# First attention of a four-layer gated model: averages of normalised tokens with folded value and output weights, keys first in each step

## The chip, the cores and the metric

The kernel is one program on one core of a Trainium2 chip. A core has TensorE (matmuls), VectorE, ScalarE and GpSimd (POOL in the profile), and SyncE (SP), which here only issues transfers. Each runs its own instructions in order, and they wait for each other on semaphores. Matmul results go to PSUM, 8 banks of 512 float32 values per partition; everything else stands in SBUF, 128 partitions. The metric is the device time of the whole program in microseconds; lower is better.

## What is computed

`x` is 128 sequences of 64 tokens of width 128, `ctx` has the same shape, all float32. Four layers follow each other, each a gated cross attention and a gated feed-forward:

```python
x = x + tanh(g_xattn[0]) * L0_xattn(ctx, layernorm(x), ...)
x = x + tanh(g_ffn[0])   * L0_ffn(layernorm(x), ...)
...
```

The change touches the first line. Its attention takes, per sequence, queries from 64 latents (the normalised `x`) and keys and values from 128 tokens (64 of `ctx`, 64 latents):

```python
xn = layer_norm(ctx, gamma_x, beta_x)         # context tokens
ln = layer_norm(layernorm(x), gamma_l, beta_l)  # latents
q = ln @ Wq                                   # 8 heads of 64
k = rope(xn @ Wk) for context tokens, ln @ Wk for latents
v = concat(xn, ln) @ Wv
out = softmax(q k^T / 8) v @ Wo               # 512 -> 128
```

Rotation (rope) of a key needs each half of a head's 64 values multiplied by the cosine, and the other half, with a sign, by the sine.

## The kernel before

Tokens are worked in 64 tiles; a tile is two sequences (`PAIR`, index b), 128 tokens on 128 partitions. `flamingo` runs `prepare` (loads and weight preparation) and then eight stages, each a loop over tiles written per engine. The stage of the change is `attention0`. All of `x` stays in SBUF (`k.x`); each stage adds to it in place, and the next stage starts when all tiles of the one before are updated.

Within a stage `steps(engine, T, lead, lag, body)` writes the software pipeline: `body(at)` is called once per step s, and `at(k)` gives the tile s + k (or nothing outside the range). Between a few written-out steps at either end it is a loop of two steps. So the order of the work on each engine is the order of the `if t := at(k)` blocks in its `body`, written out by hand, and a wait such as `pe.wait_ge(*s["krot"](t))` holds everything behind it on that engine. `t.has(2)` and `t.back(2)` name the tile two before, whose buffer or bank is used again.

In a step of `attention0` before:

- SP loads the context tile s+3 (L459), stores the latents' second affine image z1T (L462) and the transposed context (L464) of tile s+1 for a later attention, and swaps partition halves of the keys with two transfers of 64 rows, `kr` from `kc` (L469).
- POOL makes variance plus epsilon and its power -0.5 for tile s+2 (L483, L484, L487).
- TensorE: scores of s (L502), the normalised heads of s-1 turned (L510), keys (L518) and queries (L524) of s+1, three transposes of s+2 (L534 to L536), output product of s-1 (L540), weights of s turned (L550), values of s+1 (L559), weights times values of s (L569). The last has an added column of ones, so that each head's sum of weights comes with it.
- VectorE: statistics of s+2 (L583 to L588), reciprocal and normalising of the heads of s-1 (L592, L594), maximum of the scores and their difference (L602, L604, once per b), xhat (L217, in the helper `tile_xhat`) and zhat (L610) of s+2, keys times cosine (L616), three affines of the turned tokens (L626), the update of x (L630), queries into a block form with zeros `QBD` (L636), keys times sine (L642) and the sum into `KT` (L645).
- ScalarE: exponentials (L656, one per b), copies out of PSUM: `oT` (L661), `kc` (L666), `KT` of the latents (L670), the turned context (L676), the turned weights (L680), the values (L685).

Heads stand in `wq0` and `wk0` with their halves rearranged by VectorE in `prepare`, so that one swap of partition halves serves two heads.

## Time and profile before

| | |
|---|---|
| median of 3 runs | 2354.29 us (2352.95 to 2356.11) |
| the profiled execution, its own time | 2353.34 us |
| its span, first to last instruction | 2351.0 us |
| TensorE busy in the span | 2061.7 us (88%) |
| VectorE | 1836.1 us (78%) |
| ScalarE | 1189.1 us (51%) |
| GpSimd | 263.0 us (11%) |
| mean granted TensorE clock | 0.945 of 2.4 GHz |

The span is the time from the first to the last instruction of one execution on the chip; its own time lies 2.3 us above it. A float32 matmul appears as two records (x16 for 8 matmuls). The recorded busy time of a matmul includes its way through the array, which overlaps the next one; so groups are better read from start to start. `x128` is a count, `<-` in a name reads "from", and at the end of a line stands how long the engine had been idle and what released it.

### The profile page before, as it was taken

What the parts mean: (1) busy time and instruction counts of PE and PEld (TensorE: products, weight loads), DVE (VectorE), ACT (ScalarE), POOL (GpSimd) and SP (SyncE); (2) the same over time, 40 slices, a digit from 0 to 9 for tenths busy, and PEclk for the clock granted to TensorE, in tenths of its full rate; (3) what the DMA queues carried; (4) which work ended last, traced back from release to release, by engine and by line L of the source; (5) the groups of instructions that cost most, each with busy time, mean ns of one, the idle gap of its engine ahead of it and who ended that gap; (6) DMA issues with size and microseconds to landing.
All of it is one profiled execution on the core that took longest, in us unless ns stands there. A gap on an engine that the chain in (4) does not pass through costs nothing. (4 is left out here: it accounts for less than half of the span.)

```text
span 2351.0 us, 51476 instructions
## 1 busy us (share of the span) xinstructions
PE 2061.7 (88%) x17149; PEld 1603.8 (68%) x17149; DVE 1836.1 (78%) x4821; ACT 1189.1 (51%) x2276; POOL 263.0 (11%) x552
## 2 busy tenths in 40 slices
PE   3999999999977999999998978799999985599507
PEld 3888888888867986777775756477777764244207
DVE  3898899889867978888886778567666578787885
ACT  2454555555442217767765645445444445318647
POOL 0111101111101101111101124000000022100000
PEclk8999999999998999999998989799999998799859
DMA  6111111111114541111100011221221110002532
GB/s 181 44 45 47 47 47 47 45 44 44 47 26 186 233 165 26 23 23 25 24 19 1 0 33 42 84 97 72 86 94 72 73 46 28 1 0 107 189 133 71
DMA packets 121398, 153.68 MB, mean 65 GB/s; under 512 B 45513, under 2 KB 102242, under 8 KB 117218
## 3 DMA queue, kind: packets, MB, share of 16 engines
q1 hardware_dynamic: 115320, 149.92, 19.9%
q10 hardware_dynamic: 5994, 2.70, 0.4%
q8 instruction: 45, 0.74, 0.1%
q14 instruction: 39, 0.32, 0.0%
HBM read 110.11 MB, written 25.69 MB: 58 GB/s over the span
## 5 line engine op out<-in xcount | busy, mean ns | idle before, releaser
L1726 DVE TENSOR_TENSOR arena<-arena 128x512 f32<-128x512 f32 (+1 forms) x256 | 171.2, 687 | 64.4 <-ACT arena L1764 61.2
L1764 ACT ACTIVATE arena<-banks,b1c 128x512 f32<-128x512 f32 x192 | 131.7, 687 | 168.3 <-PE banks L1639 168.1
L656 ACT ACTIVATE arena<-arena 128x512 f32<-128x512 f32 x128 | 80.7, 630 | 192.9 <-DVE arena L604 192.9
L1649 PEld LDWEIGHTS banks<-w2a,arena 128*128 128x128 f32 x1024 | 124.1, 192 | 28.7 <-issue 28.7
L909 PE MATMUL banks<-we,arena 128*128 128x128 f32 x1024 | 132.9, 285 | 3.4 <-DVE arena L973 0.5
L502 PE MATMUL banks<-arena 128*128 128x128 f32 x1024 | 131.3, 281 | 0.1
L909 PEld LDWEIGHTS banks<-we,arena 128*128 128x128 f32 x1024 | 123.9, 197 | 10.2 <-DVE arena L973 9.6
L1214 ACT ACTIVATE arena<-arena 128x512 f32<-128x512 f32 x128 | 80.7, 631 | 98.5 <-DVE arena L1166 98.5
L1092 PE MATMUL banks<-arena 128*128 128x512 f32 x256 | 126.0, 615 | 3.9 <-ACT arena L1220 0.3
L1160 DVE TENSOR_REDUCE arena<-banks 128x8 f32<-128x512 f32 x128 | 87.8, 686 | 51.5 <-PE banks L1092 51.4
L518 PE MATMUL banks<-arena,wk 128*128 128x128 f32 x1024 | 126.3, 277 | 1.1 <-DVE arena L626 1.1
L559 PE MATMUL banks<-wv,arena 128*128 128x512 f32 x256 | 123.0, 603 | 2.0 <-ACT arena L676 2.0
L1649 PE MATMUL banks<-w2a,arena 128*128 128x128 f32 x1024 | 124.7, 275 | 0.0
L502 PEld LDWEIGHTS banks<-arena 128*128 128x128 f32 x1024 | 119.1, 191 | 5.3 <-DVE arena L645 0.9
L518 PEld LDWEIGHTS banks<-arena,wk 128*128 128x128 f32 x1024 | 120.8, 194 | 1.5 <-DVE arena L626 1.5
L1639 PE MATMUL banks<-arena,w1s 128*128 128x512 f32 x256 | 121.7, 610 | 0.0
L1854 PE MATMUL banks<-konst,local_max 128*1 128x128 f32 (+1 forms) x4 | 1.4, 346 | 119.6 <-DVE local_max L1838 119.6
L217 DVE TENSOR_SCALAR xhat<-x_tiles,mean_var,rstd 128x128 f32 (+1 forms) x256 | 78.8, 339 | 32.0 <-POOL rstd L762 26.7
L762 POOL TENSOR_TENSOR rstd<-var_eps,konst 128x4 f32<-128x4 f32 x96 | 100.2, 1044 | 15.0 <-POOL var_eps L759 11.6
L759 POOL TENSOR_SCALAR var_eps<-mean_var 128x4 f32<-128x4 f32 x96 | 22.5, 234 | 704.7 <-DVE mean_var L739 702.5
L569 PEld LDWEIGHTS banks<-arena 128*64 128x64 f32 x2048 | 65.0, 137 | 48.8 <-issue 47.8
L626 DVE TENSOR_SCALAR arena<-banks,affine_columns 128x128 f32<-128x128 f32 x192 | 67.0, 404 | 36.5 <-PE banks L536 36.4
(273 smaller groups left out, 5254.1 us busy)
## 6 DMA issues: line engine op xcount, KB each, us to landing
arena<-coef_scratch SPq DMA_DIRECT2D x32, 2048.0 KB, 7.0
arena<-arena SPq DMA_DIRECT2D x128, 128.0 KB, 2.3
gated_scratch<-arena SPq DMA_DIRECT2D x16, 768.0 KB, 3.2
arena<-gated_scratch SPq DMA_DIRECT2D x16, 768.0 KB, 4.3
arena<-z1T_scratch SPq DMA_DIRECT2D x128, 64.0 KB, 2.2
arena<-ctxT_scratch SPq DMA_DIRECT2D x32, 256.0 KB, 2.8
arena<-in_ctx SPq DMA_DIRECT2D x64, 64.0 KB, 1.8
z1T_scratch<-arena SPq DMA_DIRECT2D x64, 64.0 KB, 1.5
```

Source lines behind the costliest of these rows:

```text
L502: mm = pe.matmul(ps[:, 6 + b, c * P:(c + 1) * P], QBD[:, c, b].rearrange("p h i -> p (h i)"), KT[:, c, :, b, :], start=True, stop=True)
L518: mm = pe.matmul(ps[:, n, c * P:(c + 1) * P], k.wk0[:, c * P:(c + 1) * P], Z[t.par][:, :, n], start=True, stop=True)
L559: mm = pe.matmul(ps[:, 4 + b, :], Z[t.par][:, b].rearrange("p s i -> p (s i)"), k.wv0[:, :], start=True, stop=True)
L656: act.activation(prob[:, b], prob[:, b], ACT.Exp, scale=HD0 ** -0.5).then_inc(s["prob"].sem, 1)
L762: pool.tensor_tensor(k.rstd[:, :, 0], k.ve[:, :, 0], k.konst[:, C_MHALF:C_MHALF + GROUP], ALU.pow).then_inc(f["rstd_ready"].sem, GROUP)
L909: mm = pe.matmul(ps[:, OUT + g.par, j * D:(j + 1) * D], xs[g.par][:, n, j * P:(j + 1) * P], k.we0[:, n, :], start=n == 0, stop=n == EXPERT ...
L1092: pe.matmul(ps[:, 3 + n, :], QB[t.par][:, n].rearrange("p b i -> p (b i)"), KM[t.par][:, n].rearrange("p h i -> p (h i)"), start=True, sto ...
L1160: dve.tensor_reduce(mx[:, n], ps[:, 3 + n, :].rearrange("p (h i) -> p h i", i=SEQ), AX.X, ALU.max)\
L1639: pe.matmul(ps[:, HID + c % NHID, :], w, xTg[g.par], start=True, stop=True).then_inc(s["h_psum"].sem, 1)
L1649: mm = pe.matmul(ps[:, OUT + g.par, j * D:(j + 1) * D], hT[g.par][:, c, j * P:(j + 1) * P], w, start=c == 0, stop=c == CHUNKS2 - 1)
L1726: dve.tensor_tensor(hT[g.par][rows, c, :], hT[g.par][rows, c, :], wide_coef[g.par][rows, e, :], ALU.mult).then_inc(s["scaled"].sem, 1)
L1764: act.activation(hT[g.par][:, c, :], ps[:, HID + c % NHID, :], ACT.Gelu, bias=k.b1c[:, c:c + 1])\
```

## The change

`attention0` is rewritten, with what it needs in `prepare`:

- Values are no longer computed per tile. Per head, Wv Wo is folded once at the start (`wvo0`, 8 products of 128 by 128). Per tile the normalised tokens (both kinds, `Z`) are turned back into rows (`zn`), the softmax weights average them (two products of 512 columns, result `Y`), and eight accumulating products with `wvo0` give the output.
- The weights are normalised before they are turned: a sum, a reciprocal and a multiplication on VectorE. The exponentials read the scores in PSUM with minus the maximum as the bias operand, one instruction per head pair.
- Keys come first in TensorE's step. `KT` has a second buffer. The output product of s-1 goes to bank 0 (`KC`), where the next step's first key product goes too; VectorE updates x with it as the first thing of the next step (`steps(dve, T, 2, 2, body)`).
- The z1T affine is made on ScalarE. `QBD` is cleared once by POOL and filled by two ScalarE copies.
- The keys' halves are no longer rearranged in the weights; the swap is of neighbouring blocks of 32 rows, four transfers.
- The transposed context is an input made on the host (`ctxT`), and so is the transposed Wv (`wvT`); the stage no longer turns or stores the context.

The diff, cut to its core (removed lines of the bodies are in the listing above):

```diff
+    gates_raw = raw(8)
+    k.wq0, k.wk0 = (sb(n, [P, INNER]) for n in ("wq0", "wk0"))
...
+        (k.wq0[:, :], a["L0_xattn_Wq"]), (k.wk0[:, :], wkv[:, 0:INNER]), (wvT, a["wvT"]),
+        (wo_raw, a["L0_xattn_Wo"].rearrange("(c p) d -> p c d", p=P)),
         (k.we0[:, :, :], a["L0_ffn_We"].rearrange("e d m -> d e m")),
...
         act.activation(k.bout[:, :], ps[:, 7, D:2 * D], ACT.Copy, scale=k.gates[:, 2:3]).then_inc(folded_sb, 1)
+        act.wait_ge(folded, 3)
+        for n in range(2):
+            act.activation(k.wvo0[:, n::2, :], ps[:, n, :].rearrange("p (h d) -> p h d", d=D), ACT.Copy)\
...
         pe.matmul(ps[:, 7, D:2 * D], k.konst[0:1, C_ONES:C_ONES + P], bo_row[0:1, :], start=False, stop=True)\
             .then_inc(folded, 1)
+        for h in range(H0):
+            rows = slice(h % 2 * HD0, h % 2 * HD0 + HD0)
+            mm = pe.matmul(ps[:, h % 2, h // 2 * D:(h // 2 + 1) * D], wvT[rows, h // 2, :], wo_raw[rows, h // 2, :],
+                           start=True, stop=True)
...
+    mx, nb, ssum, rec = (k.take(PAIR * HPAIRS).rearrange("p (b c) -> p b c", b=PAIR) for _ in range(4))
+    prob = k.take(PAIR * 512).rearrange("p (b c n) -> p b c n", b=PAIR, c=HPAIRS)
+    probT = k.take(PAIR * 512).rearrange("p (b n) -> p b n", b=PAIR)
...
         def body(at):
             if t := at(3):
                 if t.has(2):
+                    sp.wait_ge(*s["zhat"](t.back(2)))
+                    k.hold(sp)
                 sp.dma_start(cin[t.par], ctx_dram[t.idx]).then_inc(ctx_loaded.at(t), 16)
             if t := at(1):
                 sp.wait_ge(*s["kc"](t))
+                k.hold(sp)
                 if t.has(1):
                     sp.wait_ge(*s["ksin"](t.back(1)))
+                    k.hold(sp)
+                for n in range(4):
+                    to, of = n * 32, (n ^ 1) * 32
+                    sp.dma_start(kr[to:to + 32, :], kc[of:of + 32, :]).then_inc(swapped.at(t), 16)
+                sp.wait_ge(*s["z1"](t))
+                k.hold(sp)
+                sp.dma_start(k.z1T_dram[t.idx], z1o[t.par]).then_inc(k.z1T_stored.at(t), 16)
...
+        pool.memset(QBD, 0.0).then_inc(preset, 1)
...
+        def body(at):
+            if t := at(1):
+                if t.has(3):
+                    pe.wait_ge(*f["x_updated"](t.back(3)))
+                if t.has(1):
+                    pe.wait_ge(*s["klat"](t.back(1)))
+                for n in range(2):
+                    pe.wait_ge(*s["z_ready"](t, n + 1))
+                    for c in range(HPAIRS):
+                        mm = pe.matmul(ps[:, KC + n, c * P:(c + 1) * P], k.wk0[:, c * P:(c + 1) * P], Z[t.par][:, :, n],
+                                       start=True, stop=True)
+                    mm.then_inc(s["k_psum"].sem, 1)
+            if t := at(-1):
+                for b in range(PAIR):
+                    pe.wait_ge(*s["normed"](t, b + 1))
+                    if t.has(1):
+                        pe.wait_ge(*s["y_sb"](t.back(1), b + 1))
+                    for c in range(HPAIRS):
+                        mm = pe.transpose(ps[:, PT + b, c * P:(c + 1) * P], prob[:, b, c], k.ident)
+                    mm.then_inc(s["pt_psum"].sem, 1)
             if t := at(0):
                 pe.wait_ge(*s["krot"](t))
                 pe.wait_ge(*s["klat"](t))
                 pe.wait_ge(*s["qbd"](t))
+                if t.has(1):
+                    pe.wait_ge(*s["prob"](t.back(1)))
                 for b in range(PAIR):
                     for c in range(HPAIRS):
+                        mm = pe.matmul(ps[:, S + b, c * P:(c + 1) * P], QBD[:, c, b].rearrange("p h i -> p (h i)"),
+                                       KT[t.par][:, c, :, b, :], start=True, stop=True)
                     mm.then_inc(s["s_psum"].sem, 1)
+                if at(1):
+                    pe.wait_ge(*s["z1"](at(1)))
+                for b in range(PAIR):
+                    mm = pe.transpose(ps[:, TURN, (2 + b) * P:(3 + b) * P], Z[t.par][:, b].rearrange("p s i -> p (s i)"),
+                                      k.ident)
+                mm.then_inc(s["zn_psum"].sem, 1)
             if t := at(-1):
+                pe.wait_ge(*s["zn_sb"](t))
+                for b in range(PAIR):
+                    pe.wait_ge(*s["pt_sb"](t, b + 1))
+                    pe.matmul(ps[:, PT + b, :], zn[t.par][:, b], probT[:, b], start=True, stop=True)\
+                        .then_inc(s["y_psum"].sem, 1)
+            if t := at(1):
+                if t.has(1):
+                    pe.wait_ge(*s["qbd"](t.back(1)))
                 for c in range(HPAIRS):
+                    mm = pe.matmul(ps[:, Q, c * P:(c + 1) * P], k.wq0[:, c * P:(c + 1) * P], Z[t.par][:, :, 1],
                                    start=True, stop=True)
                 mm.then_inc(s["q_psum"].sem, 1)
             if t := at(2):
                 pe.wait_ge(*f["xhat_ready"](t))
                 pe.wait_ge(*s["zhat"](t))
+                if at(0):
+                    pe.wait_ge(*s["zn_sb"](at(0)))
+                if at(1):
+                    pe.wait_ge(*s["z1"](at(1)))
+                pe.transpose(ps[:, TURN, 0:P], k.xh[:, t.par, :], k.ident)
+                pe.transpose(ps[:, TURN, P:2 * P], zh[t.par], k.ident).then_inc(f["xT_psum"].sem, 1)
             if t := at(-1):
+                pe.wait_ge(*s["y_sb"](t))
                 if at(1):
                     pe.wait_ge(*s["kc"](at(1)))
+                elif t.has(1):
+                    pe.wait_ge(*f["x_updated"](t.back(1)))
                 for h in range(H0):
+                    mm = pe.matmul(ps[:, KC, 0:D], Y[:, h].rearrange("p b i -> p (b i)"), k.wvo0[:, h, :],
+                                   start=h == 0, stop=h == H0 - 1)
...
+        def normalise(t, b):
+            dve.wait_ge(*s["prob"](t, (b + 1) * HPAIRS))
+            dve.tensor_reduce(ssum[:, b], prob[:, b], AX.X, ALU.add).then_inc(s["ssum"].sem, 1)
+            dve.wait_ge(*s["ssum"](t, b + 1))
+            dve.reciprocal(rec[:, b], ssum[:, b]).then_inc(s["srec"].sem, 1)
+            dve.wait_ge(*s["srec"](t, b + 1))
+            dve.tensor_tensor(prob[:, b], prob[:, b], rec[:, b].unsqueeze(2).broadcast_to([P, HPAIRS, P]), ALU.mult)\
+                .then_inc(s["normed"].sem, 1)
+        def body(at):
+            if t := at(-2):
+                dve.wait_ge(*s["out_psum"](t))
+                dve.scalar_tensor_tensor(out=k.x[:, t.idx, :], in0=ps[:, KC, 0:D], scalar=k.gates[:, 0:1],
+                                         in1=k.x[:, t.idx, :], op0=ALU.mult, op1=ALU.add)\
+                    .then_inc(f["x_updated"].sem, 1)
+            if t := at(-1):
+                normalise(t, 1)
...
             if t := at(1):
                 if t.has(1):
                     dve.wait_ge(*s["krot"](t.back(1)))
                 dve.wait_ge(*s["kc"](t))
                 dve.tensor_tensor(rotA.rearrange("p (c i) -> p c i", i=SEQ), kc.rearrange("p (c i) -> p c i", i=SEQ),
...
+            if t := at(0):
+                for b in range(PAIR):
+                    dve.wait_ge(*s["s_psum"](t, b + 1))
+                    dve.tensor_reduce(mx[:, b], ps[:, S + b, :].rearrange("p (c n) -> p c n", c=HPAIRS), AX.X, ALU.max)\
+                        .then_inc(s["smax"].sem, 1)
+                    dve.wait_ge(*s["smax"](t, b + 1))
+                    if t.has(1):
+                        dve.wait_ge(*s["prob"](t.back(1)))
+                    dve.tensor_scalar(nb[:, b], mx[:, b], -HD0 ** -0.5, None, ALU.mult).then_inc(s["nb"].sem, 1)
             if t := at(1):
                 dve.wait_ge(*swapped(t))
                 dve.tensor_tensor(rotB.rearrange("p (c i) -> p c i", i=SEQ), kr.rearrange("p (c i) -> p c i", i=SEQ),
                                   sinT, ALU.mult).then_inc(s["ksin"].sem, 1)
                 dve.wait_ge(*s["ksin"](t))
+                dve.wait_ge(*s["kcos"](t))
+                if t.has(2):
+                    dve.wait_ge(*s["s_psum"](t.back(2)))
+                dve.tensor_tensor(KT[t.par][:, :, 0], rotA.rearrange("p (c b i) -> p c b i", c=HPAIRS, b=PAIR),
                                   rotB.rearrange("p (c b i) -> p c b i", c=HPAIRS, b=PAIR), ALU.add)\
                     .then_inc(s["krot"].sem, 1)
+            if t := at(2):
+                sl = t.par
+                if t.has(2):
+                    dve.wait_ge(*f["xT_psum"](t.back(2)))
+                tile_xhat(k, f, dve, t, sl)
+                dve.tensor_scalar(zh[sl], cin[sl], k.mv[:, sl, 1, 0:1], k.rstd[:, sl, 1:2],
+                                  ALU.subtract, ALU.mult).then_inc(s["zhat"].sem, 1)
+            if t := at(0):
+                normalise(t, 0)
+            if t := at(2):
+                sl = t.par
+                if t.has(2):
+                    dve.wait_ge(*s["zn_psum"](t.back(2)))
+                    dve.wait_ge(*s["q_psum"](t.back(2)))
+                dve.wait_ge(*f["xT_psum"](t))
+                for dst, n, g in ((Z[sl][:, :, 0], 1, 0), (Z[sl][:, :, 1], 0, 2)):
+                    dve.tensor_scalar(dst, ps[:, TURN, n * P:(n + 1) * P].rearrange("p (b i) -> p b i", b=PAIR),
+                                      k.aff[:, g:g + 1], k.aff[:, g + 1:g + 2],
+                                      ALU.mult, ALU.add).then_inc(s["z_ready"].sem, 1)
+        steps(dve, T, 2, 2, body)
...
         def body(at):
             def weights(b):
                 if t := at(0):
+                    act.wait_ge(*s["nb"](t, b + 1))
+                    if t.has(1):
+                        act.wait_ge(*s["pt_psum"](t.back(1), b + 1))
+                    for c in range(HPAIRS):
+                        act.activation(prob[:, b, c], ps[:, S + b, c * P:(c + 1) * P], ACT.Exp, scale=HD0 ** -0.5,
+                                       bias=nb[:, b, c:c + 1]).then_inc(s["prob"].sem, 1)
+            def average(b):
+                if t := at(-1):
+                    if t.has(1) and b == 0:
+                        act.wait_ge(*s["out_psum"](t.back(1)))
+                    act.wait_ge(*s["y_psum"](t, b + 1))
+                    act.activation(Y[:, :, b, :], ps[:, PT + b, :].rearrange("p (h i) -> p h i", i=SEQ), ACT.Copy)\
+                        .then_inc(s["y_sb"].sem, 1)
             if t := at(1):
+                act.wait_ge(*s["z_ready"](t))
+                if t.has(2):
+                    act.wait_ge(*k.z1T_stored(t.back(2)))
+                act.activation(z1o[t.par], ps[:, TURN, P:2 * P], ACT.Identity, scale=k.aff[:, 4:5],
+                               bias=k.aff[:, 5:6]).then_inc(s["z1"].sem, 1)
                 act.wait_ge(*s["k_psum"](t, 1))
                 if t.has(1):
+                    act.wait_ge(*s["kcos"](t.back(1)))
+                    act.wait_ge(*swapped(t.back(1)))
+                act.activation(kc, ps[:, KC, :], ACT.Copy).then_inc(s["kc"].sem, 1)
+                act.wait_ge(*s["k_psum"](t))
+                if t.has(2):
+                    act.wait_ge(*s["s_psum"](t.back(2)))
+                act.activation(KT[t.par][:, :, 1], ps[:, KL, :].rearrange("p (c b i) -> p c b i", c=HPAIRS, b=PAIR),
+                               ACT.Copy).then_inc(s["klat"].sem, 1)
+            if t := at(-1):
+                for b in range(PAIR):
+                    act.wait_ge(*s["pt_psum"](t, b + 1))
+                    act.activation(probT[:, b], ps[:, PT + b, :], ACT.Copy).then_inc(s["pt_sb"].sem, 1)
+            weights(0)
+            average(0)
+            if t := at(0):
+                act.wait_ge(*s["zn_psum"](t))
+                if t.has(2):
+                    act.wait_ge(*s["y_psum"](t.back(2)))
+                act.activation(zn[t.par].rearrange("p b d -> p (b d)"), ps[:, TURN, 2 * P:4 * P], ACT.Copy)\
+                    .then_inc(s["zn_sb"].sem, 1)
+            average(1)
             weights(1)
             if t := at(1):
+                act.wait_ge(*s["q_psum"](t))
+                if t.has(1):
+                    act.wait_ge(*s["s_psum"](t.back(1)))
+                for h in range(2):
+                    rows = slice(64 * h, 64 * h + 64)
+                    act.activation(QBD[rows, :, :, h, :].rearrange("p c b i -> p (c b) i"),
+                                   ps[rows, Q, :].rearrange("p (n i) -> p n i", i=SEQ), ACT.Copy)\
...
+    c[:, C_SIN:C_SIN + SEQ] *= np.where(np.arange(P) // (HD0 // 2) % 2 == 0, -1, 1)[:, None]
     c[:, C_IOTA:C_IOTA + EXPERTS] = np.arange(EXPERTS)
...
-    for name, a in list(inputs.items()) + [("shape_constants", shape_constants())]:
+    tiles = np.asarray(inputs["ctx_1024"]).reshape(-1, P, D)
+    wv = np.asarray(inputs["L0_xattn_Wkv"])[:, INNER:].reshape(D, HPAIRS, P)
+    laid_out = [("shape_constants", shape_constants()), ("ctxT", tiles.transpose(0, 2, 1)),
+                ("wvT", wv.transpose(2, 1, 0))]
+    for name, a in list(inputs.items()) + laid_out:
```

## Rows read from the trace of the kernel before

**Rows 1.** Busy time, engine by engine, with granted clock, DMA share and GB/s.

```profile
60.00:680.00 620.00, 620.00 (x6131) 539.44 (x6131) 556.57 (x1230) 312.49 (x617) 65.91 (x183) 1.00 0.19 46
```

**Rows 2.** TensorE in order of time, one step: start, duration, line, operation.

```profile
409.54 1.92 PE L559 MATMUL banks<-wv,arena 128*128 128x512 f32 x4
411.39 1.15 PE L569 MATMUL banks<-arena 128*64 128x65 f32 x32
412.48 2.05 PE L502 MATMUL banks<-arena 128*128 128x128 f32 x16
414.37 0.60 PE L510 MATMUL banks<-konst,arena 128*128 128x128 f32 x4
414.80 1.95 PE L518 MATMUL banks<-arena,wk 128*128 128x128 f32 x16
416.59 1.06 PE L524 MATMUL banks<-arena,wq 128*128 128x128 f32 x8
...
417.81 1.06 PE L540 MATMUL banks<-wo,arena 128*128 128x128 f32 x8
418.70 1.04 PE L550 MATMUL banks<-konst,arena 128*128 128x128 f32 x8
419.58 1.92 PE L559 MATMUL banks<-wv,arena 128*128 128x512 f32 x4
```

**Rows 3.** VectorE in order of time, from a step of the same stage.

```profile
408.05 1.05 DVE L626 TENSOR_SCALAR arena<-banks,affine_columns 128x128 f32<-128x128 f32 x3 [0.56 <-PE banks L536]
409.01 0.34 DVE L630 SCALAR_TENSOR_TENSOR x_tiles<-banks,gates,x_tiles 128x128 f32 x1
409.27 1.21 DVE L636 TENSOR_TENSOR arena<-banks,konst 128x1024 f32<-128x1024 f32 x1
410.40 0.68 DVE L642 TENSOR_TENSOR arena<-arena,konst 128x512 f32<-128x512 f32 x1
411.12 0.69 DVE L645 TENSOR_TENSOR arena<-arena 128x512 f32<-128x512 f32 x1
411.75 0.29 DVE L583 BATCH_NORM_STATS2 bn_parts<-arena 128x6 f32<-128x128 f32 x1
...
412.59 0.21 DVE L592 RECIPROCAL arena<-banks 128x8 f32<-128x8 f32 x1
```

**Rows 4.** Groups by line and shape, whole span: busy, mean ns, then idle before.

```profile
L602 DVE TENSOR_REDUCE arena<-banks 128x4 f32<-128x512 f32 x128 | 87.7, 685 | 9.5 <-PE banks L502 0.5
L666 ACT ACTIVATE arena<-banks 128x512 f32<-128x512 f32 x64 | 37.7, 589 | 1.8 <-PE banks L518 1.8
L1237 ACT ACTIVATE arena<-banks,affine_columns 128x128 f32<-128x128 f32 x64 | 30.2, 472 | 25.3 <-PE banks L1153 25.3
L350 ACT ACTIVATE bout<-banks,gates 128x128 f32<-128x128 f32 x1 | 0.4, 361 | 0.0
```

**Rows 5.** Transfers: SP's queue in one step, and the page's list (KB, us to landing).

```profile
406.72 1.11 SPq L469 DMA_DIRECT2D arena<-arena  x2
...
arena<-arena SPq DMA_DIRECT2D x128, 128.0 KB, 2.3
```

**Rows 6.** The start of the stage in order of time, TensorE and VectorE.

```profile
43.09 3.49 PE L518 MATMUL banks<-arena,wk 128*128 128x128 f32 x16 [1.14 <-DVE arena L626]
...
50.65 0.69 DVE L645 TENSOR_TENSOR arena<-arena 128x512 f32<-128x512 f32 x1
...
51.40 2.05 PE L502 MATMUL banks<-arena 128*128 128x128 f32 x16
```

**Rows 7.** The end of the stage in order of time, TensorE and VectorE.

```profile
683.01 2.05 PE L502 MATMUL banks<-arena 128*128 128x128 f32 x16
...
693.13 1.16 PE L540 MATMUL banks<-wo,arena 128*128 128x128 f32 x8 [0.69 <-ACT arena L661]
...
694.33 0.35 DVE L630 SCALAR_TENSOR_TENSOR x_tiles<-banks,gates,x_tiles 128x128 f32<-128x128 f32 x1 [2.60 <-PE banks L540]
```

**Rows 8.** A stretch of a later stage, busy times and clock as in the first group.

```profile
1400.00:1420.00 20.00, 17.76 (x163) 14.21 (x162) 19.01 (x83) 12.04 (x23) 9.83 (x12) 1.00 0.19 55
```

More of the change, by code:

```diff
@@ L411, in ready @@
         eng.wait_ge(gates_ready, 2)
[L412 to L413 removed]
+        eng.wait_ge(built, 1)
+        eng.wait_ge(turned_sb, 11)
         eng.wait_ge(folded_sb, 5)
@@ L421, in attention0 @@
 def attention0(k, no):
-    nc, ps, T = k.nc, k.psum, k.T
+    ps, T = k.psum, k.T
     f = k.front(no)
@@ L429, in attention0 @@
     Z = [z.rearrange("p (b s i) -> p b s i", b=PAIR, s=2) for z in two(2 * P)]
-    z1o, cto = two(P), two(P)
-    KT = k.take(HPAIRS * 4 * SEQ).rearrange("p (c s b i) -> p c s b i", c=HPAIRS, s=2, b=PAIR)
+    zn = [z.rearrange("p (b d) -> p b d", b=PAIR) for z in two(PAIR * D)]
+    z1o = two(P)
+    KT = [v.rearrange("p (c s b i) -> p c s b i", c=HPAIRS, s=2, b=PAIR) for v in two(HPAIRS * 4 * SEQ)]
     kc, kr = k.take(512), k.take(512)
@@ L529, in body @@
                 pe.wait_ge(*s["zhat"](t))
-                if t.has(1):
-                    pe.wait_ge(*s["ctxT_sb"](t.back(1)))
-                if t.has(2):
-                    pe.wait_ge(*s["v_sb"](t.back(2)))
-                pe.transpose(ps[:, 4, 0:P], k.xh[:, t.par, :], k.ident)
-                pe.transpose(ps[:, 4, P:2 * P], zh[t.par], k.ident)
-                pe.transpose(ps[:, 4, 2 * P:3 * P], cin[t.par], k.ident).then_inc(f["xT_psum"].sem, 1)
-            if t := at(-1):
-                pe.wait_ge(*s["ot_sb"](t))
-                for c in range(HPAIRS):
-                    mm = pe.matmul(ps[:, 5, 0:D], oT[:, c * P:(c + 1) * P], k.wo0[:, c, :],
-                                   start=c == 0, stop=c == HPAIRS - 1)
-                mm.then_inc(s["out_psum"].sem, 1)
@@ L552, in body @@
-            if t := at(1):
-                if at(2):
-                    pe.wait_ge(*s["z_ready"](at(2)))
-                    pe.wait_ge(*s["ctxT_sb"](at(2)))
-                if at(-1):
-                    pe.wait_ge(*f["x_updated"](at(-1)))
-                for b in range(PAIR):
-                    mm = pe.matmul(ps[:, 4 + b, :], Z[t.par][:, b].rearrange("p s i -> p (s i)"), k.wv0[:, :],
-                                   start=True, stop=True)
-                    mm.then_inc(s["v_psum"].sem, 1)
```

165 lines of the change are left out of this document (16 added, 149 removed).

## The prediction

> **What bounds the kernel now.** I first asked for the busy time of each engine over the stage of the first attention, which is the only stage that the change rewrites. In 620 us of it TensorE is busy 620.00 us, VectorE 556.57, ScalarE 312.49, GpSimd 65.91, at a granted clock of 1.00 (2.4 GHz) [rows 1]. So a step is as long as TensorE's work in it. Next, TensorE in order of time through one step [rows 2]: from one V product (L559) to the next it is 10.04 us, and each group starts when the one before has been issued. VectorE in the same step [rows 3] works about 9 us and waits once, 0.56 us, for the turned tiles (L626). From the first scores (51.40) to the last (683.01) there are 63 steps in 631.61 us [rows 6, 7]: 10.03 us each.
>
> I use start-to-start distances, not busy times: 8 matmuls of 128 columns take 1.79 us (L518), 4 take 0.89, a transpose 0.11 (8 in 0.88, L550), a 512-column matmul 0.925 (L559, 1.85 for two). The tail of a group is recorded 0.17 us past the last distance (1.06 busy against 0.89).
>
> **TensorE's work.** Removed per step: V (1.85), weights times V (L569, 1.09), turning the normalised heads (L510, 0.43), the old output product (0.89), one of the three transposes of tokens (0.11). Added: two transposes of the normalised tokens (0.22), two 512-column products of tokens and weights (1.85), an output product of 8 matmuls instead of 4 (1.78). The scores lose 0.10: L502 takes 1.89 where L518 takes 1.79 for the same shape, and its first matmul comes right after the 64-row products that go. Sum: keys 1.79, weights turned 0.88, scores 1.79, tokens turned 0.22, averages 1.85, queries 0.89, tokens of step+2 turned 0.22, output 1.78: **9.42 us**, 0.61 less than now. Alone that would be 63 x 0.61 = 38 us.
>
> **The wait that takes its place.** The new key product writes bank 0, which also holds the output product of the tile before last. So the first instruction of TensorE's step waits for `x_updated`, VectorE's first instruction of the same step, and that waits for the output product, the last of TensorE's step before. Nothing is between them in TensorE's queue. The price is in the last tile of the stage and the first one: the output product's end at 694.29, the update from 694.33 (0.04 later) for 0.35 [rows 7]; the rotated keys' end at 51.34 and TensorE's next start at 51.40, 0.06 later [rows 6]; and a group after a wait is 0.10 longer (1.16 for 8 records against 1.06) [rows 2, 7]. Tail 0.17 + 0.04 + 0.35 + 0.06 + 0.10 = 0.72 us. TensorE's step is then 9.42 + 0.72 = 10.14, already longer than 10.03. Behind the waiting key product on TensorE's queue stands everything.
>
> **Walking one new step.** Zero is the first key matmul; a handoff is taken as 0.05. First keys done 1.16, ScalarE copies them out (0.59, L666) until 1.80 [rows 4]. TensorE: keys to 1.89, weights turned to 2.77, scores of b=0 to 3.66 (recorded 3.83), b=1 to 4.56 (4.73), tokens turned 4.78, averages 6.63, queries 7.52. It now needs xhat and zhat of tile step+2.
>
> VectorE: the update from -0.41, then the normalising of b=1 (a sum like L602's 0.69 [rows 4], a reciprocal like L592's 0.21, a multiplication like L645's distance 0.63, with 0.04 before each dependent one, as between L642 and L645 [rows 3]), 1.6 us, in time for the transposes of b=1 at 2.33; statistics 0.84; keys times cosine. All done near 3.0; it waits for scores. Maximum of b=0 at 3.88, its negative 0.73 later (4.61, 0.18 like L592's small tile), maximum of b=1 at 4.79, negative at 5.52, free at 5.70. Then keys times sine, which needs the swapped keys; the sum 0.72 later; xhat 0.63 later; zhat 0.26 later for 0.34 [rows 3]. Starting at 5.70, zhat is ready at 7.65 and TensorE, due at 7.52, waits 0.18.
>
> The **swap** is now four DMAs of 32 rows instead of two of 64. SP issues the present two in 1.11 us, and one lands 2.3 us after issue [rows 5]; now they are far from any reader's wait. There is no row for a 32-row one. Lower bound: proportional to rows, 0.28 each, the last landing at 5.0. Upper: 0.56 each, so the last is issued at 1.85 + 1.67 = 3.52 and lands at 5.82, sine at 5.87. I take the upper one, the row's own price per instruction. Then the sum is at 6.59, xhat 7.22, zhat 7.48 to 7.82, TensorE turns them from 7.87 (0.35 idle) to 8.15 (0.06 for starting afresh), output to 9.93 (recorded 10.10), update 10.15 to 10.50, next keys at 10.55. VectorE has normalised b=0 by 9.35 and written Z by 9.99, just before the update. **Step 10.55**; with the swap in time, 10.38.
>
> On this the Trainium skill (DMA: Bandwidth & Descriptors, Rules for kernel authors) speaks against the split: transfers to disjoint partition halves use the same engines, so splitting wins nothing. The rows here show one size only and cannot say it; by that rule the four take at least what the two took, which leaves the step between 10.38 and 10.55.
>
> ScalarE: the exponentials of one b are now 4 instructions instead of one, 0.36 each with a per-partition operand (L350) [rows 4], 1.44; from 4.84 they end 6.3, the copy of averages 0 by 6.9, tokens 7.3, averages 1 at 7.9, before the output product at 8.15. The z1 affine, moved here from VectorE, runs before the keys are done. Queries' copies end near 10.5, wanted by the scores at 13.3. Hidden, with 0.2 us of margin. Lost margin would lengthen the step one for one.
>
> SP: the context load now waits for zhat and still has a step; the z1T store stands behind the four swaps, and its reader is the next attention. The ctxT store (64 KB a tile) is gone, nobody waited for it. POOL's three instructions per tile are unmoved; its one clearing of QBD lies beside the first context load. The four weight copies at the start go (-0.8), but eight folding products (0.43 each at the low clock, as the first key products: 8 in 3.49 [rows 6], 3.4) and two copies (1.1) come at the end of the preparation, of which about 2.5 us is left after the overlap: bounds 1.5 and 3.7.
>
> **Ends of the stage.** Keys of tile 0 start at 43.09, scores at 51.40 [rows 6], 8.3 later. In the new order the first keys are copied out 2.7 after their start (half of 3.49, 0.2, handoff, 0.6), swapped (1.7 and 2.3: 6.8), rotated (8.1), the next tile is normalised and turned (9.1), its affines made and keys computed (11.7): +3.4, less 0.3 for the third affine. The first interval lacks averages and output (-0.3), the last lacks keys (-0.7). Drain: from the last scores 11.7 us now (683.01 to 694.68) [rows 7]; new: scores and averages of the tile before 4, exponentials 1.8, normalising 1.7, transposes and copy 1.2, averages 1.0, copy 0.65, output 1.95, update 0.4, 12.8: +1.1. Sum with the preparation: 2.5 + 3.1 - 1.0 + 1.1 = **5.7 us**.
>
> **The sum.** 63 x (10.55 - 10.03) = 32.8, plus 5.7: +38.5 us on the profiled execution's own 2353.3, **2391.8 us**. The median of the runs shown is 1 us higher. Other stages read the same bytes and stay. A measurement of this kernel can tell 0.2%, 4.7 us, from no change.
>
> **Rivals.**
> Swap in time (the split costs nothing): step 10.38, 2353.3 + 22.1 + 5.7 = **2381**. For it: the low bound of the issue. Chance 0.25.
> Only the handoff at the step's boundary: xhat is never late, 10.14, **2366**. Against it: VectorE's chain behind the scores is 3.8 us of measured durations. 0.10.
> **Faster.** The update is hidden and TensorE's work alone decides: 9.42, 2353 - 38.4 + 5.7 = **2320**. It needs the 0.72 to vanish and xhat early; it decides from a step under 9.86 (10.4 us less over 63 steps, of which the ends take 5.7 and 4.7 are left). Against it: both waits are in the program's order, and VectorE's own distances, read off the walk, already add to 9.3. 0.10. Between that and the handoff case, unchanged within 0.2%: 0.06.
> Heavier: exponentials and averages late on ScalarE (at 0.47 each, L1237's price with two operands [rows 4], the last copy would miss 8.15 by 0.2 us), or register waits between VectorE's many small instructions (0.05 on six of them, 0.3): 10.7 to 10.9, **2400 to 2414 us**, 0.09.
> The clock drops: TensorE now pauses twice a step. The rows are against it: at 17.76 us busy in 20 it stayed 1.00 [rows 8]. Were one step in twenty at the lower level, 1.2 GHz, its 9.4 us of work would double: +30 us on the forecast, **2422**, 0.02. The Trainium skill (TensorE: Matmul & The Clock Gate, A second HAM failure mode: psum-queue depth-cycling) reports a clock that swings with frequent short pauses between groups of matmuls; rows 8 do not show that.
> My forecast: 0.38.
>
> Slower by over 0.2%: 0.38 + 0.25 + 0.10 + 0.09 + 0.02 = 0.84; same 0.06; faster 0.10. The range leaves out the faster case and part of the heavier one, and takes in the bounds of the swap and of the preparation: 2363 to 2406.
>
> **What would show it.** In the new profile: TensorE idle about 0.5 us before the keys, released by the update; idle 0.2 to 0.4 before the transposes of xhat; VectorE idle near 0.9 before the first maximum; sine idle on a DMA (forecast) or never (first rival); ScalarE 7 to 8 us busy per step. If TensorE stays 100% busy, I am wrong on the side of the faster case.

## The result and the profile after

The changed kernel takes 2412.7 us (median of 4 runs, 2409.62 to 2414.02) against 2355.2 us (4 runs): ratio 1.0241, 95% interval 1.0223 to 1.0258. It is slower, as forecast, but by 57.5 us instead of 38.5, and 7 us above the upper end of the range (2406). The profiled execution took 2409.62 us with a span of 2407.8, 56.8 more than before.

First, one step of the changed kernel in order of time. TensorE (start, duration, line, operation, idle before and its releaser):

```profile
402.57 2.05 PE L509 MATMUL banks<-arena,wk 128*128 128x128 f32 x16 [0.75 <-DVE x_tiles L586]
404.45 1.04 PE L518 MATMUL banks<-konst,arena 128*128 128x128 f32 x8
405.32 1.95 PE L528 MATMUL banks<-arena 128*128 128x128 f32 x16
407.11 0.38 PE L534 MATMUL banks<-konst,arena 128*128 128x128 f32 x2
407.33 1.88 PE L541 MATMUL banks<-arena 128*128 128x512 f32 x4
409.05 1.05 PE L547 MATMUL banks<-arena,wq 128*128 128x128 f32 x8
410.56 0.30 PE L557 MATMUL banks<-konst,xhat 128*128 128x128 f32 x1 [0.45 <-DVE xhat L216]
...
410.80 1.95 PE L566 MATMUL banks<-wvo,arena 128*128 128x128 f32 x16
413.39 2.05 PE L509 MATMUL banks<-arena,wk 128*128 128x128 f32 x16 [0.64 <-DVE x_tiles L586]
```

VectorE in the same step:

```profile
401.99 0.35 DVE L586 SCALAR_TENSOR_TENSOR x_tiles<-banks,gates,x_tiles 128x128 f32 x1 [0.29 <-PE banks L566]
...
406.42 0.69 DVE L610 TENSOR_REDUCE arena<-banks 128x4 f32<-128x512 f32 x1 [1.10 <-PE banks L528]
...
408.52 0.69 DVE L618 TENSOR_TENSOR arena<-arena,konst 128x512 f32<-128x512 f32 x1 [0.31 <-DMA arena<-arena]
409.25 0.69 DVE L624 TENSOR_TENSOR arena<-arena 128x512 f32<-128x512 f32 x1
...
410.11 0.34 DVE L632 TENSOR_SCALAR arena<-arena,mean_var,rstd 128x128 f32<-128x128 f32 x1
...
412.90 0.35 DVE L586 SCALAR_TENSOR_TENSOR x_tiles<-banks,gates,x_tiles 128x128 f32 x1 [0.28 <-PE banks L566]
```

TensorE, never idle before [rows 1], pauses twice: 0.45 us before xhat (L557; 0.36 in the next step) and 0.64 or 0.75 us, in turn, before the keys (L509), each time for VectorE. Its groups have the lengths that were added up: from L509 to L518 1.88 with the late first matmul, then 0.87, 1.79, 0.22, 1.72 (forecast 1.85); the issue of the output product (L566) shows only where nothing is waited for behind it, in e1 and e3 below: 1.79 and 1.80. VectorE pauses too, 1.10 us for the scores, 0.31 for the swapped keys (L618), 0.28 or 0.29 for the output product. No engine is full: each waits for the other in turn, which is what a closed chain of waits (one that leads back to its own start, one step later) would look like. Whether it is one, the experiments test.

The busy times of a stretch of the stage (columns as in [rows 1]) and SP's four swap transfers, with their way to landing from the view of that line:

```profile
400.00:500.00 100.00, 89.40 (x665) 77.48 (x663) 81.30 (x205) 66.39 (x166) 12.23 (x27) 1.00 0.15 36
```

```profile
404.66 2.42 SPq L474 DMA_DIRECT2D arena<-arena  x4
```

```profile
L474 SPq DMA_DIRECT2D arena<-arena x256: 507/584/1439, 46.3 to 731.0; - x128
...
DMA to landing us min/median/max: 1.9/2.0/2.9
```

TensorE is down from 100% to 89%, ScalarE up from 50% to 66%, the granted clock stays at 1.00 although TensorE pauses twice a step. Issuing a 32-row transfer costs SP 0.58 us (median 584 ns), as a 64-row one did (two in 1.11 us [rows 5]).

**Where the 56.8 us are.** Scores of tile 0 start at 57.14 us (51.40 before), those of tile 63 at 739.07 (683.01), and x of the last tile is updated at 753.27 (694.68). So 5.7 us come before the first scores, 50.3 over the 63 steps (681.93 against 631.61), 2.5 in the drain; the other stages, whose code is the same, are 1.8 us shorter. From the eighth key product to the 62nd of 64, keys follow keys after 10.81 to 10.90 us; before them, single steps take up to 11.8.

### The profile page after: what moved, and what is told of

Its sections match the earlier page's. It is cut to its first block and busy times, and to the rows that moved or that the text cites. A ratio compares the mean times of both kernels' runs of the same rounds, so it can differ in the third digit from the quotient of the medians.

```text
span 2407.8 us, 49851 instructions
## 1 busy us (share of the span) xinstructions
PE 2048.0 (85%) x15437; PEld 1589.4 (66%) x15437; DVE 1820.7 (76%) x4945; ACT 1327.0 (55%) x2790; POOL 280.0 (12%) x551
## 5 line engine op out<-in xcount | busy, mean ns | idle before, releaser
L659 ACT ACTIVATE arena<-banks,arena 128x128 f32<-128x128 f32 x512 | 146.1, 372 | 70.0 <-DVE arena L615 70.0
L509 PE MATMUL banks<-arena,wk 128*128 128x128 f32 x1024 | 135.5, 287 | 44.2 <-DVE x_tiles L586 41.6
L509 PEld LDWEIGHTS banks<-arena,wk 128*128 128x128 f32 x1024 | 123.3, 197 | 56.5 <-DVE arena L643 52.0
L610 DVE TENSOR_REDUCE arena<-banks 128x4 f32<-128x512 f32 x128 | 88.6, 692 | 72.3 <-PE banks L528 72.3
L1236 ACT ACTIVATE arena<-arena 128x512 f32<-128x512 f32 x128 | 80.7, 631 | 95.2 <-DVE arena L1188 95.2
L1114 PE MATMUL banks<-arena 128*128 128x512 f32 x256 | 125.1, 611 | 1.5 <-ACT arena L1242 0.3
L566 PE MATMUL banks<-wvo,arena 128*128 128x128 f32 x1024 | 125.1, 275 | 1.4 <-ACT arena L667 1.4
L528 PE MATMUL banks<-arena 128*128 128x128 f32 x1024 | 125.4, 276 | 0.0
L566 PEld LDWEIGHTS banks<-wvo,arena 128*128 128x128 f32 x1024 | 119.4, 192 | 3.0 <-ACT arena L667 3.0
L541 PE MATMUL banks<-arena 128*128 128x512 f32 x256 | 120.5, 593 | 0.0
```

Source lines behind the costliest of these rows:

```text
L509: mm = pe.matmul(ps[:, KC + n, c * P:(c + 1) * P], k.wk0[:, c * P:(c + 1) * P], Z[t.par][:, :, n], start=True, stop=True)
L528: mm = pe.matmul(ps[:, S + b, c * P:(c + 1) * P], QBD[:, c, b].rearrange("p h i -> p (h i)"), KT[t.par][:, c, :, b, :], start=True, stop=True)
L541: pe.matmul(ps[:, PT + b, :], zn[t.par][:, b], probT[:, b], start=True, stop=True)\
L566: mm = pe.matmul(ps[:, KC, 0:D], Y[:, h].rearrange("p b i -> p (b i)"), k.wvo0[:, h, :], start=h == 0, stop=h == H0 - 1)
L659: act.activation(prob[:, b, c], ps[:, S + b, c * P:(c + 1) * P], ACT.Exp, scale=HD0 ** -0.5, bias=nb[:, b, c:c + 1]).then_inc(s["prob"].se ...
L1114: pe.matmul(ps[:, 3 + n, :], QB[t.par][:, n].rearrange("p b i -> p (b i)"), KM[t.par][:, n].rearrange("p h i -> p (h i)"), start=True, sto ...
```

## The experiments

All start from the changed kernel except the one that says otherwise. The question was what a step of 10.83 us consists of, since the forecast had 10.55, and whether its two pauses are one chain or two independent losses.

**e1_output_bank: the boundary wait alone.**

```diff
@@ tensor, keys of s+1
-                if t.has(3):
-                    pe.wait_ge(*f["x_updated"](t.back(3)))
@@ tensor, weights of s-1 turned
+                if t.has(1):
+                    pe.wait_ge(*f["x_updated"](t.back(1)))
@@ tensor, output product of s-1
-                if at(1):
-                    pe.wait_ge(*s["kc"](at(1)))
-                elif t.has(1):
-                    pe.wait_ge(*f["x_updated"](t.back(1)))
...
-                    mm = pe.matmul(ps[:, KC, 0:D], Y[:, h].rearrange("p b i -> p (b i)"), k.wvo0[:, h, :],
+                    mm = pe.matmul(ps[:, PT, 0:D], Y[:, h].rearrange("p b i -> p (b i)"), k.wvo0[:, h, :],
```

(The update of x reads `ps[:, PT, 0:D]` too.)

> The changed kernel with one part moved: the output product of a tile goes to the bank of the turned weights (PT, free once the averages of b=0 are copied) instead of the keys' bank, so the key product no longer waits for the update of x; the next turning of the weights does. My theory: a step of the changed kernel (10.83 us) is one closed chain, keys, swap, sine, sum, xhat, zhat, turned tokens, output product, update, keys; its piece from the output product's issue to the next key product (tail 0.17, handoff 0.15, update 0.35, handoff 0.14) goes, the wait for xhat stays. Step 10.0 us, 61 steps save 0.8 each: about 2364 us. Rival (the wait at the boundary only takes the place of a wait for xhat that would come anyway): the pause of TensorE before xhat's transposes grows by what is saved and the step stays over 10.5: 2395 or more.

Measured: 2354.01 us (10 runs, 2348.85 to 2358.16), ratio to the kernel before 0.9994 (0.9983 to 1.0004): 58.7 us below the changed kernel, all that it had lost, and 10 us less than expected. TensorE around the boundary:

```profile
410.92 0.30 PE L557 MATMUL banks<-konst,xhat 128*128 128x128 f32 x1 [0.29 <-DVE xhat L216]
...
411.17 1.95 PE L562 MATMUL banks<-wvo,arena 128*128 128x128 f32 x16
412.96 1.95 PE L507 MATMUL banks<-arena,wk 128*128 128x128 f32 x16
```

The keys now follow the output product after 1.79 us, its issue alone, and the pause before xhat did not grow; it shrank, to 0.29. The step is 9.83 and 9.93 us in turn. The rival falls. The step went below the expected 10.0 because that pause shrank too. The keys, no longer behind a wait, are on their way sooner: SP starts the swap 1.86 us after the first key matmul (404.97 after 403.11) instead of 2.09. The sine then starts 0.32 us after the last minus-maximum instruction, against 0.48 in the changed kernel; without any wait it is 0.12 (e4 below), so the swap is still a little late. A step of 9.88 is already shorter than the 10.03 of the kernel before; the total is the same because the stage's start and end are longer (5.6 us more before the first scores and 2.5 more behind the last, as in the changed kernel).

**e2_xhat_early: the late xhat alone.**

```diff
@@ vector, after nb
+            if t := at(2):
+                sl = t.par
+                if t.has(2):
+                    dve.wait_ge(*f["xT_psum"](t.back(2)))
+                tile_xhat(k, f, dve, t, sl)
+                dve.tensor_scalar(zh[sl], cin[sl], k.mv[:, sl, 1, 0:1], k.rstd[:, sl, 1:2],
+                                  ALU.subtract, ALU.mult).then_inc(s["zhat"].sem, 1)
             if t := at(1):
                 dve.wait_ge(*swapped(t))
...
-            if t := at(2):
-                sl = t.par
-                if t.has(2):
-                    dve.wait_ge(*f["xT_psum"](t.back(2)))
-                tile_xhat(k, f, dve, t, sl)
-                dve.tensor_scalar(zh[sl], cin[sl], k.mv[:, sl, 1, 0:1], k.rstd[:, sl, 1:2],
-                                  ALU.subtract, ALU.mult).then_inc(s["zhat"].sem, 1)
```

> The changed kernel with VectorE's xhat and zhat of tile s+2 placed before the keys times sine, so behind neither the swap nor the rotation. My theory: TensorE no longer waits before the transposes of xhat (0.45 us), the boundary wait stays: step 10.2 us, about 2374 us; the sine no longer waits for the swap. Rival (only the boundary counts): step unchanged, 2412 us. Rival (VectorE is the bound, its order does not matter): unchanged too, with VectorE at no idle.

Measured: 2372.22 us (4 runs, 2370.27 to 2375.74), ratio to the kernel before 1.0077 (1.006 to 1.0094), 40.5 below the changed kernel. TensorE:

```profile
410.14 0.27 PE L557 MATMUL banks<-konst,xhat 128*128 128x128 f32 x1
...
410.36 1.95 PE L566 MATMUL banks<-wvo,arena 128*128 128x128 f32 x16
412.94 2.05 PE L509 MATMUL banks<-arena,wk 128*128 128x128 f32 x16 [0.63 <-DVE x_tiles L586]
```

The pause before xhat is gone, the one before the keys (0.63 and 0.75 in turn) is all that is left, step 10.17 and 10.29. The order on VectorE does matter, against both rivals.

**e4_two_swaps: the price of the split.** Rows 64 to 127 are not swapped.

```diff
-                for n in range(4):
+                for n in range(2):
```

(`keys_swapped` counts two, and POOL clears `kr` once.)

> The changed kernel with two of the four swap transfers left out (rows 64 to 127 of the swapped keys stay zero, so rotated keys of those rows are not those of the reference). My theory: the swap's issue on SP, 0.6 us each, ends later than VectorE is free, and the sine's wait of 0.31 and 0.22 us on alternate steps is on the closed chain: step 0.27 us shorter, about 2396 us. Rival (a swap in time, the wait is absorbed elsewhere): 2412 us.

Measured: 2386.81 us (4 runs, 2382.04 to 2390.93), 25.9 below the changed kernel and 9 below what was expected. The steady steps take 10.45 and 10.56 us, 0.33 less than 10.83; over 61 steps that is 20 us. In the two profiles all 63 steps together are 21.8 us shorter, among them a first one of the changed kernel that takes 11.60 us from sine to sine with a wait of 1.10 for the swap, and the first scores start 1.9 us sooner. Another 3.8 us of the spans' difference lie behind the last scores, where the edit changed nothing. VectorE in this kernel, minus the maximum and then the sine:

```profile
404.51 0.17 DVE L616 TENSOR_SCALAR arena<-arena 128x4 f32<-128x4 f32 x1
404.63 0.69 DVE L619 TENSOR_TENSOR arena<-arena,konst 128x512 f32<-128x512 f32 x1
```

0.12 us apart, no wait. So the last two transfers were on the chain, and the rival of a swap in time falls. This run stands in for a swap by two transfers of 64 rows: two issues of 32 rows take SP 1.15 us, the old pair took 1.11, but the old pair moved twice the bytes and landed 2.3 us after issue instead of 2.0.

**e5_written_out: why the handoffs were longer than forecast.** `steps` writes all 67 steps of the stage out; every wait is then on a constant and there is no loop.

```diff
-    if end - first < 4:
+    if flat or end - first < 4:
@@ attention0, all five engines
-        steps(pe, T, 2, 1, body)
+        steps(pe, T, 2, 1, body, flat=True)
```

> The changed kernel with all steps of the first attention written out instead of a loop of two steps, so that every wait is on a constant. The prediction took 0.05 us for a handoff between engines, from rows outside the loop; inside it the profile of the changed kernel shows 0.11 to 0.15 where an engine stands waiting. Theory A (waits on register values cost it): the handoffs fall back to 0.05, the step from 10.83 to about 10.55, 2395 us. Theory B (handoffs under load are longer whatever the wait): unchanged, 2412 us, and a longer time if fetching more instructions costs.

Measured: 2403.28 us (4 runs, 2400.76 to 2407.98), 9.4 below the changed kernel, less than theory A's 17. One of its steps, TensorE and VectorE, and SP's queue in that step and in the one before:

```profile
410.79 1.95 PE L566 MATMUL banks<-wvo,arena 128*128 128x128 f32 x16
412.78 0.35 DVE L586 SCALAR_TENSOR_TENSOR x_tiles<-banks,gates,x_tiles 128x128 f32<-128x128 f32 x1 [0.16 <-PE banks L566]
413.19 2.05 PE L509 MATMUL banks<-arena,wk 128*128 128x128 f32 x16 [0.44 <-DVE x_tiles L586]
...
419.04 0.69 DVE L618 TENSOR_TENSOR arena<-arena,konst 128x512 f32<-128x512 f32 x1 [0.21 <-DMA arena<-arena]
...
421.32 1.95 PE L566 MATMUL banks<-wvo,arena 128*128 128x128 f32 x16
423.31 0.35 DVE L586 SCALAR_TENSOR_TENSOR x_tiles<-banks,gates,x_tiles 128x128 f32<-128x128 f32 x1 [0.16 <-PE banks L566]
423.72 0.49 PE L509 MATMUL banks<-arena,wk 128*128 128x128 f32 x2 [0.45 <-DVE x_tiles L586]
```

```profile
403.94 3.14 SPq L474 DMA_DIRECT2D arena<-arena  x4
...
415.15 2.41 SPq L474 DMA_DIRECT2D arena<-arena  x4
```

Both theories hold a part. A handoff is the time from the end of one engine's instruction to the start of another's that waits for it. The output product ends at 412.74 and the update starts at 412.78; the update ends at 413.13 and the keys start at 413.19: 0.04 and 0.06 us, the two numbers that the prediction had read outside the loop [rows 6, 7]. In the loop they are 0.15 (412.75 to 412.90) and 0.14 (413.25 to 413.39) in one step and 0.17 (401.82 to 401.99) and 0.23 (402.34 to 402.57) in the other. This step is 10.53 us long. But 19 of 58 steps (the first three and the last two left aside) take 10.8 to 12.0, 15 us more together than at 10.5: in the step from 401.98 to 413.19 the swap took SP 3.14 us, and the sine waited 0.89. Written out, one issue took up to 1.68 us. The transfers that fetch instructions, between 100 and 600 us, first of the changed kernel (queue, packets, MB, share), then written out:

```profile
q14 instruction: 2, 0.02, 0.0%
q8 instruction: 1, 0.02, 0.0%
```

```profile
q8 instruction: 27, 0.44, 0.4%
q14 instruction: 26, 0.21, 0.1%
```

The trace ties the long issues to these fetches. Between 50 and 740 us, 15 of the 376 issues on SP took over 0.8 us, and each of the 15 began within 0.5 us of the start of a 16 KB transfer on q8; of the other 361, none took more than 0.60 us. The changed kernel has two such issues in its first steps, both beside such a transfer; the longer of the two (1.44 us) is behind the wait of 1.10 above. That the fetch makes the issue long is what fits; no run took the fetches away.

Where the longer handoff comes from, the trace shows in part. Two groups of the changed kernel, which this kernel's trace does not have (PEldq is the queue of weight loads, DVEq that of VectorE; durations in ns):

```profile
L507 PEldq FUSED_REGOPS  x58: 37/37/42, 98.1 to 716.6; - x58
L586 DVEq FUSED_REGOPS  x58: 64/70/89, 97.5 to 716.1; - x58
```

There are 58 of each, one for each of the loop's 58 steps. In the loop a register instruction takes the wait (TensorE's at 413.29, 0.04 us after the update's end), and the first weights load behind it, at 413.38; written out, that load itself takes the wait, at 413.19. In every second step, the one that begins the loop's body, TensorE has two register instructions there (402.38 and 402.48, the load at 402.56), and the handoff is 0.23 instead of 0.14. So theory A is right about the size: steps with the swap in time fall from 10.83 to 10.51 us. Late transfers take most of it back.

**e7_before_written_out: the same on the kernel before.** The edit of e5 on the kernel before.

> The kernel before with all steps of its first attention written out. TensorE was never idle there, so register waits cost it nothing: 2354 us, unchanged within 0.2 per cent. If writing out itself costs (fetch of instructions), it shows here as 2360 us or more.

Measured: 2357.68 us (10 runs, 2353.52 to 2360.36), ratio 1.0009 (1.0000 to 1.0019): unchanged within 0.2%. A handoff's wait costs nothing where TensorE is never idle. Writing out is still not quite free: from the first scores to the last the profile shows 635.22 us against 631.61, because each step takes TensorE 10.09 us instead of 10.03, the difference standing around its V product (from L550 to L569 2.79 against 2.72). The kernel before has the same 10.10 in the few steps that it writes out itself.

**e3_bank_and_xhat: both moves.** The diffs of e1 and e2 together.

> The changed kernel with both moves: output product in the bank of the turned weights, xhat and zhat before the sine. Each alone took the step from 10.83 to 9.88 and to 10.17 us. My theory: both pieces of the chain are gone, TensorE's own 9.42 us and a wait of 0.1 to 0.2 for the normalised weights of b=1 are left: step 9.55, about 2335 us, and less than the kernel before. Rival (VectorE, whose distances add to 9.1 and which still hands over four times a step, decides): step 9.7 to 9.9, 2343 to 2355 us, TensorE idle more than 0.3 us a step.

Measured: 2324.16 us (5 runs, 2320.85 to 2330.46), ratio to the kernel before **0.9869** (0.9851 to 0.9887). It beats both. Busy times, then the scores of two neighbouring steps on TensorE:

```profile
100.00:600.00 500.00, 499.36 (x3816) 444.35 (x3815) 461.15 (x1166) 381.79 (x954) 71.49 (x160) 1.00 0.17 42
```

```profile
400.59 1.95 PE L528 MATMUL banks<-arena 128*128 128x128 f32 x16
...
409.99 1.95 PE L528 MATMUL banks<-arena 128*128 128x128 f32 x16
```

TensorE is busy again without a gap (499.36 of 500 us), and from scores to scores it is 9.40 and 9.45 us in turn. The rival in which VectorE decides falls. The two moves alone took 0.95 and 0.60 us off the step, both together 1.41. So the two pauses were pieces of one chain, and what is taken out of it adds up until TensorE's own work decides.

**e6_both_written_out.** e3 and e5 together.

> The kernel with both moves and all steps of the stage written out. Written out, the changed kernel had steps of 10.51 us (the prediction's 10.55) wherever the swap was in time, and steps of 11 to 12 where one issue of the swap on SP took over 1 us. With xhat before the sine the swap is behind more work. My theory: the long issues are mostly covered, the shorter handoffs gain at most 0.05 a step, 2332 to 2340 us. Rival (fetching written-out code costs on every engine): 2345 us or more.

Measured: 2341.05 us (4 runs, 2339.23 to 2341.84), ratio 0.9937 (0.9922 to 0.9953), 17 us above e3 and just above the 2340 that I had allowed. Most steps are 9.46 us, where the loop of e3 has 9.40 and 9.45, and 20 of 63 are 9.85 to 10.6, 14 us more together. All 18 issues on SP over 0.8 us again begin within 0.5 us of a 16 KB instruction transfer, and VectorE then waits for the swap (17 times between 100 and 600 us, 10.2 us in all). Short handoffs gain nothing here. For this kernel the loop is the better form.

**e8_both_two_swaps.** e3 with the edit of e4.

> The kernel with both moves and two of the four swap transfers left out (rows 64 to 127 of the swapped keys stay zero). My theory: the swap is off the chain once xhat does not stand behind it, so the two transfers are worth nothing now: the same time as with both moves alone, within 3 us. Rival (the transfers cost by themselves, by SP's queue or by traffic, wherever the sine stands): 10 to 20 us less.

Measured: 2318.75 us (4 runs, 2316.89 to 2324.61), 5.4 below e3, whose runs overlap it. The steady steps are the same, 9.40 and 9.45. In the two profiles (spans 2322.7 and 2327.1) 4.2 us of the difference lie in the first seven steps, 66.4 against 70.6 us from keys to keys, where the sine still waits with four transfers (0.74 and 0.70 us, and 2.87 against 1.57 for the first tile). So the two transfers cost nothing in the steady state once xhat does not stand behind them, and some 4 us at the start, a little more than I had expected.

## Why the prediction was right in kind and short in size

The walked step, from the key product on, against two neighbouring steps of the changed kernel (keys at 402.57 and at 413.39) and the undisturbed step of e5 (413.19):

| | forecast | changed kernel | its next step | written out |
|---|---|---|---|---|
| SP issues the first swap | 1.85 | 2.09 | 1.96 | 1.96 |
| sine starts | 5.87 | 5.95 | 5.86 | 5.85 |
| zhat done | 7.82 | 7.88 | 7.79 | 7.78 |
| output product starts | 8.15 | 8.23 | 8.14 | 8.13 |
| update of x starts | 10.15 | 10.33 | 10.26 | 10.12 |
| next keys | 10.55 | 10.82 | 10.84 | 10.53 |

**The wait that takes its place** was right: e1 removes it alone and gets all the loss back. Its price was too low, and that is the step of the prediction that failed: the two handoffs at the boundary, taken as 0.04 and 0.06 from the first and last tiles of the stage, which are written out, where the loop has 0.15 and 0.14 in one step and 0.17 and 0.23 in the next. By the table, from the output product to the next keys was forecast as 2.40; it is 2.59 and 2.70 in the loop and 2.40 written out. Up to the output product the walk is 0.08 short in one step and exact in the other. Together the step is 0.27 to 0.29 longer; over 61 steps that is 17 us of the 18 by which the total was too small. A row of the loop was there to read: VectorE's affines [rows 3] began at 408.05, 0.11 after the last transpose before them had ended:

```profile
407.67 0.27 PE L536 MATMUL banks<-konst,arena 128*128 128x128 f32 x1
```

**The swap** came out right at the end that was taken, the sine at 5.95 and 5.86 instead of 5.87, but by two errors that offset each other: SP began it 0.11 to 0.24 later and needed 0.605 us instead of 0.56 for each of the four, and they landed after 2.0 us instead of 2.3. e4 puts the price of two transfers more at 0.33 us a step, where the forecast had 0.17 for the split: the sine moves up by the whole wait. The Trainium skill (DMA: Bandwidth & Descriptors, Rules for kernel authors), cited there, says that splitting over partition halves wins nothing. This case agrees: four issues take SP 2.42 us, two took 1.11.

**TensorE's work**, 9.42 us as a sum of start-to-start distances, is what e3 runs at (9.40). The gain of 0.6 us a step was real all the time. That the sum is so close is partly luck: in e3 the averages take 1.72 instead of 1.85 and the keys 1.89 instead of 1.79. The 0.10 that L502 takes longer than L518 [rows 2] was expected to go with the 64-column products; it shows up at the keys instead, for a reason that no run shows.

**ScalarE** stayed hidden, as said: four exponentials took 1.15 us together, less than the 1.44 allowed, and its last copy for the output product ended at 409.85, 0.95 before that product.

**The ends** came to 5.7 before the first scores, where the forecast had 5.6, but by other parts, so that is luck. The preparation was put at 2.5; the stage's first transposes came 1.3 us later than before and its first keys 0.4, because the folding products took 16 records in 1.16 us at a granted clock of 1.00, where 3.4 us had been put down at the low clock. The second key products ran at 0.50 (3.75 us), after TensorE had stood idle for 3.69 us around the first swap. The granted clock of 39 to 60 us is 0.62, against 0.83 before. The drain cost 2.5, not 1.1. The forecast had nothing for VectorE's order in it: the exponentials of the last tile's b=1 end at 744.63, but the update of the tile before stands ahead of their normalising, and waits until 745.73 for its output product; the normalising starts at 746.00.

**The rivals.** A swap in time, and the handoff alone, are out by e4 and by the profile. The case of more small waits (2400 to 2414) is where the time landed, though not on ScalarE and not at VectorE's small instructions, which follow each other after 0.03 to 0.04 us as forecast, but at the boundary itself. I had given it 0.09 with the reason "register waits"; e5 and the register instructions in the trace bear that reason out, in another place. The clock did not drop: it is 1.00 from 68.7 us to the end of the stage, with two pauses of 0.4 and 0.7 us in each 10.8 us. The Trainium skill (TensorE: Matmul & The Clock Gate, A second HAM failure mode: psum-queue depth-cycling) tells of a clock that swings, in another kernel, with frequent short pauses between groups of matmuls; here it did not show. The faster case lacked only its condition, that the update is hidden and xhat early. e3 makes both true and gets 2324 us, where that rival had said 2320.

## What to carry to other kernels

When a reordering lets a bank or buffer be taken over at the seam between two steps, write down who frees it and what that one waits for: here the last product of a step, one VectorE instruction and the first product of the next made a closed chain, and it cost 59 us of 2413 while TensorE's own work had become 0.6 us a step shorter. A free bank for that product gave the 59 back. Read handoff times from inside the loop where they will occur, not from its written-out ends. And look at which products stand behind a transfer in an engine's order without needing it: moving 0.6 us of VectorE's work from behind the swap to before it was worth 30 to 40 us.

## What the runs showed of the hardware

- A handoff between engines where the second stands waiting took 0.04 (TensorE to VectorE) and 0.06 us (VectorE to TensorE) in written-out code; in the loop the same instructions took 0.15 and 0.14 us in one step and 0.17 and 0.23 in the next, with one register instruction, or on TensorE in every second step two, between the wait and the work (e5 against the changed kernel).
- Written-out code is not free. In 500 us the fetches of instructions rose from 3 to 53 packets. All 33 issues of a transfer on SP over 0.8 us (up to 1.68; e5 and e6) began within 0.5 us of the start of a 16 KB fetch, and no other issue took more than 0.60. e6 lost 17 us against the same kernel with a loop; in e7, where TensorE is never idle, a step became 0.06 us longer (10.09 against 10.03).
- A transfer of 32 rows of 2 KB from SBUF to SBUF costs SP 0.58 us to issue, the same as one of 64 rows, while one of 128 rows of 512 B from HBM costs 0.36; the rows' count did not set it. Why the two differ was not tested.
